# The last stage of a graph network: experts paired in the TensorE array, their third bias on VectorE, the last routing moved

## The reference, cut to what matters

```
x  = feat + wv @ Wp.T + bp
x  = x + gelu(layernorm(x)*g+b @ W1.T + b1) @ W2.T + b2      # MLP, 256 -> 1024 -> 256
xn = layernorm(x)
out = x + shared(xn) + sum over the 2 chosen experts of w_e * expert_e(xn)
shared:   relu(xn@sW1+sb1) 256->256, relu(.@sW2+sb2) ->128, .@sW3+sb3 ->256
expert_e: relu(xn@eW1+eb1) 256->128, relu(.@eW2+eb2) ->64,  .@eW3+eb3 ->256     # 4 experts
w: softmax over the 4 gate logits, the top 2, softmax of those two; 0 for the others
```

## Time and profile before

| | us |
|---|---|
| median of 3 runs | 3447.66 (3445.65 to 3448.48) |
| the profiled execution's own time | 3449.33 |
| its span | 3447.5 |
| busy: PE, PEld, DVE, ACT | 3052.7, 1592.6, 2646.8, 2136.7 |
| granted TensorE clock, mean | 0.965 |

### The profile page before, as it was taken

One profiled execution on the slowest core, in us unless ns is written; L12 is line 12 of the kernel. 1 busy time (PEld: TensorE's weight loads), 2 busy tenths in 40 slices (PEclk: granted clock), 3 DMA queues, 4 the chain that ended last, 5 costly groups with the idle time before them and its releaser, 6 DMA issues. The chain is left out here.

```text
span 3447.5 us, 43195 instructions
## 1 busy us (share of the span) xinstructions
PE 3052.7 (89%) x15721; PEld 1592.6 (46%) x15722; DVE 2646.8 (77%) x2631; ACT 2136.7 (62%) x2651; POOL 248.2 (7%) x379
## 2 busy tenths in 40 slices
PE   3776777898898988899879989999999999979998
PEld 3223333333333334788769853333333333267775
DVE  8998999799999997455442259999999999843433
ACT  3101479799999997111223359999999999834333
POOL 0000000000000000000035400101110101100000
PEclk9998999999999999999989999999999999989998
DMA  2000245677777764544176553333332333210000
GB/s 59 0 0 19 79 164 202 209 234 231 226 232 223 233 222 145 192 149 141 48 202 211 170 202 110 94 92 94 92 94 91 95 92 92 68 67 23 8 8 15
DMA packets 199234, 424.88 MB, mean 123 GB/s; under 512 B 35929, under 2 KB 133457, under 8 KB 199054
## 3 DMA queue, kind: packets, MB, share of 16 engines
q1 hardware_dynamic: 185518, 395.36, 35.8%
q0 software_dynamic: 13536, 27.08, 2.7%
HBM read 354.07 MB, written 61.88 MB: 121 GB/s over the span
## 5 line engine op out<-in xcount | busy, mean ns | idle before, releaser
L1002 PE MATMUL acc<-weights_then_messages,messages 128*64 128x391 f32 x3200 | 571.6, 505 | 81.1 <-DVE weights_then_messages L1067 74.2
L2126 PE MATMUL acc<-weights,keys_and_values 128*64 128x448 f32 x2096 | 451.2, 552 | 2.0 <-DVE weights L2289 1.9
L1002 PEld LDWEIGHTS acc<-weights_then_messages,messages 128*64 128x64 f32 x3200 | 221.3, 139 | 424.9 <-issue 273.2
L2113 PE MATMUL scores<-q,keys_and_values 32*128 32x448 f32 x2800 | 362.6, 587 | 9.5 <-ACT x L2249 4.5
L1064 DVE SCALAR_TENSOR_TENSOR weights_then_messages<-rho,kappa,counts 128x1564 f32<-128x1564 f32 x200 | 367.5, 1837 | 0.0
L1067 DVE TENSOR_TENSOR weights_then_messages<-weights_then_messages,counts 128x1564 f32<-128x1564 f32 x200 | 356.2, 1781 | 11.2 <-ACT weights_then_messages L1025 11.1
L1023 ACT ACTIVATE weights_then_messages<-rho,wx 128x1564 f32<-128x1564 f32 x200 | 317.8, 1589 | 33.2 <-PE acc L1002 31.2
L1025 ACT ACTIVATE weights_then_messages<-weights_then_messages,kappa 128x1564 f32<-128x1564 f32 x200 | 319.9, 1600 | 6.5
L674 PE MATMUL acc<-weights_then_messages 128*128 128x400 bf16 x1024 | 232.3, 359 | 85.3 <-ACT acc L650 44.2
L2286 DVE SCALAR_TENSOR_TENSOR weights<-weights,x 128x3584 f32<-128x3584 f32 x75 | 291.9, 3893 | 4.3 <-DVE weights L2279 1.1
L2251 ACT ACTIVATE weights<-scores 128x896 f32<-128x896 f32 x300 | 287.6, 981 | 10.2 <-PE scores L2113 10.2
(11 more groups left out here) (392 smaller groups left out, 4346.9 us busy)
## 6 DMA issues: line engine op xcount, KB each, us to landing
counts<-edge_counts SPq DMA_DIRECT2D x200, 782.0 KB, 4.5
x<-edge_counts SPq DMA_DIRECT2D x264, 224.0 KB, 2.7
edge_counts<-counts_out SPq DMA_DIRECT2D x40, 1000.0 KB, 4.2
counts<-edge_counts SPq DMA_DIRECT2D x24, 1600.0 KB, 7.9
w_first<-in_L_ffn_W_dram SPq DMA_DIRECT2D x57, 512.0 KB
counts<-edge_counts SPq DMA_DIRECT2D x86, 224.0 KB, 2.7
w_second<-in_L_ffn_W_dram SPq DMA_DIRECT2D x8, 512.0 KB, 8.0
normed_rows<-normed SPq DMA_DIRECT2D x5, 640.0 KB, 4.0
```

What stands on the lines that cost most here:

```text
L1002: ins = nc.tensor.matmul(acc[64 * q:64 * q + 64, m, 0:CP], message(t, head(r, q)), w[:, T % WR, q, m * CP:(m + 1) * CP], start=(t == 0), s ...
L2113: ins = nc.tensor.matmul(sc[:, (n + j // 2) % SR, j % 2, 0:CA], kT[part, r % KF, t * P:(t + 1) * P], q[part, r % 2, :], start=True, stop=True)
L2126: ins = nc.tensor.matmul(acc[64 * e:64 * e + 64, p, 0:CA], msg[:, t, r % KF * 2 + p, D * e:D * e + 2 * D], weights(U // 2)[:, 2 * p + e, U ...
```

## The change

1. The third layer's bias leaves the matmul. `e3_b` holds the four biases on all partitions (one DMA of 512 KB written, the first on SP's queue in this stage), and VectorE adds bias times weight in 20 instructions for each chunk (`add_expert_bias`); for chunks 0 to 3 they stand between the reads of the next chunk's MLP, for chunk 4 on both sides of the shared net's reads. The row of ones, its memset and TensorE's wait for it go.
2. Experts (0, 1) and (2, 3) are pairs. The second layers of a pair write PSUM partitions 0 to 63 and 64 to 127 of one bank (128 rows by 64 columns of the array each), and ScalarE reads both at once. The third layers of a pair use the array's rows 0 to 63 and 64 to 127, two banks of `down`, two reads on VectorE (`pair_down`, `finish_pair`).
3. The second pair's third layers of chunk c-2 are issued one tile at a time after halves 3 to 7 of `mlp_up` in iteration c, those of chunk 3 among the shared net's first layer in the last part. The first pair's are spread over the end of the experts (`end_moe`).
4. `norm(1, c+2)` on VectorE moves from before to behind `finish_mlp` for c = 1, 2, and its root on ScalarE behind the shared net's first layer. `norm(2)` is split: the second pair's reads stand between its statistics and its application.
5. Iteration 4: flips of chunk 4 after the shared second layer, its logits before the shared third layer, `route(4)` on VectorE right behind the shared net's reads, and its exponentials on ScalarE after entries 3 and 4 of the list.

```diff
-    MOE_UPS = [("s", 1), (0, 1), ("s", 2), (1, 1), (0, 2)] + [u for e in range(2, NE) for u in ((e, 1), (e - 1, 2))] + [(NE - 1, 2)]
+    SECOND_PAIR_AT = (3, 4, 5, 6, 7)
+    MOE_UPS = [("s", 1), (0, 1), ("s", 2), (1, 1), (2, 1), ("first", 2), (3, 1), ("second", 2)]
+    EXPERTS = {"first": (0, 1), "second": (2, 3)}
...
+        def pair_second(pe, c, pair, h):
+            n = up_no[("moe", c, pair, 2, 0, h)]
+            wait_up(pe, n)
+            pe.wait_ge(s_act, up_no[("moe", c, EXPERTS[pair][1], 1, 0, h)] + 1)
+            for i, e in enumerate(EXPERTS[pair]):
+                lanes = slice(i * P // 2, (i + 1) * P // 2)
+                ins = nc.tensor.matmul(up[lanes, n % RING, 0:TH], tw.e2[:, e, :], eh1[:, e, half(h)], start=True, stop=True)
+            ins.then_inc(s_up, 1)
...
+        def pair_down(pe, c, pair, j):
+            if j == 0:
+                pe.wait_ge(s_act, up_no[("moe", c, pair, 2, 0, 1)] + 1)
+            wait_down(pe, down_no[(EXPERTS[pair][1], c, j)])
+            for i, e in enumerate(EXPERTS[pair]):
+                n, lanes = down_no[(e, c, j)], slice(i * P // 2, (i + 1) * P // 2)
+                nc.tensor.matmul(down[:, n % RING, 0:F], eh2[lanes, e // 2, j * P:(j + 1) * P], tw.e3[lanes, e // 2, :],
+                                 start=True, stop=True).then_inc(s_down, 1)
...
+                if c and j < NE:                      # in finish_mlp, behind the read of tile j
+                    add_expert_bias(dve, c - 1, j)
...
+        def add_expert_bias(dve, c, e):
+            for j in range(TC):
+                ...
+                nc.vector.scalar_tensor_tensor(out=node, in0=e3_b[:, e, :], scalar=wf[:, c % 2, j, e:e + 1], in1=node,
+                                               op0=ALU.mult, op1=ALU.add).then_inc(s_eb, 1)
+        def finish_pair(dve, c, pair):
+            ...
+            for j in range(TC):
+                node = X[:, c * TC + j, :]
+                for i, e in enumerate(EXPERTS[pair]):
+                    n = down_no[(e, c, j)]
                     dve.wait_ge(s_down, n + 1)
+                    dve.wait_ge(s_read, n if i else down_no[("s", c, j) if pair == "first" else (EXPERTS["first"][1], c, j)] + 1)
+                    nc.vector.scalar_tensor_tensor(out=node, in0=down[:, n % RING, 0:F], scalar=wf[:, c % 2, j, e:e + 1],
+                                                   in1=node, op0=ALU.mult, op1=ALU.add).then_inc(s_read, 1)
...
             def _(sp):
+                sp.dma_start(e3_b[:, :, :].rearrange("p e f -> p (e f)"), a["L1_ffn_eb3"].rearrange("e f -> (e f)").partition_broadcast(P)
+                             ).then_inc(s_eb_in, 16)
...
             def _(pe):
                 pe.wait_ge(tw.sem, tw.count)
-                pe.wait_ge(s_row, 1)
...
+                def start_moe(c, with_pairs_of=None):
+                    for m in range(KF):
+                        for h in range(2):
+                            first_layer(pe, c, "s", m, h)
+                            if with_pairs_of is not None:
+                                pair_down(pe, with_pairs_of, "second", 2 * m + h)
+                    if with_pairs_of is not None:
+                        pair_down(pe, with_pairs_of, "second", TC - 1)
+                    for h in range(2):
+                        first_layer(pe, c, 0, 0, h)
+                    for h in range(2):
+                        shared_second(pe, c, h)
+                    if c == LAST_C - 1:
+                        for g in range(3):
+                            flip(pe, 2, LAST_C, g)
+                    for h in range(2):
+                        first_layer(pe, c, 1, 0, h)
+                    if c == LAST_C - 1:
+                        logits(pe, LAST_C)
+                    shared_down(pe, c)
+                def end_moe(c):
+                    for h in range(2):
+                        first_layer(pe, c, 2, 0, h)
+                    for h in range(2):
+                        pair_second(pe, c, "first", h)
+                    for h in range(2):
+                        first_layer(pe, c, 3, 0, h)
+                        if h == 1:
+                            pair_down(pe, c, "first", 0)
+                    pair_down(pe, c, "first", 1)
+                    for h in range(2):
+                        pair_second(pe, c, "second", h)
+                        pair_down(pe, c, "first", 2 + h)
+                    pair_down(pe, c, "first", 4)
...
+                        if n in SECOND_PAIR_AT and c >= 2:
+                            pair_down(pe, c - 2, "second", SECOND_PAIR_AT.index(n))
...
+                        start_moe(c - 1)
+                        end_moe(c - 1)
+                start_moe(LAST_C, with_pairs_of=LAST_C - 1)
+                end_moe(LAST_C)
+                for j in range(TC):
+                    pair_down(pe, LAST_C, "second", j)
...
             def _(dve):
-                nc.vector.memset(eh2[P // 2:P // 2 + 1, :, :], 1.0).then_inc(s_row, 1)
...
+                    if c:
+                        finish_shared(dve, c - 1)
+                        if c == LAST_C:
+                            route(dve, link, LAST_C)
+                        finish_pair(dve, c - 1, "first")
+                finish_pair(dve, LAST_C - 1, "second")
+                for e in range(NE // 2):
+                    add_expert_bias(dve, LAST_C, e)
+                finish_shared(dve, LAST_C, NE // 2)
+                for e in range(NE // 2, NE):
+                    add_expert_bias(dve, LAST_C, e)
+                finish_pair(dve, LAST_C, "first")
+                finish_pair(dve, LAST_C, "second")
```

More of the change, by code:

```diff
@@ L2397, in stage_tail @@
     for c in range(NTC + 1):
+        downs += [(e, c - 2, j) for j in range(TC) for e in EXPERTS["second"] if c >= 2]
         downs += [("proj", c + 2, j) for j in range(TC) if c + 2 < NTC]
         downs += [("mlp", c, j) for j in range(TC) if c < NTC]
-        downs += [(net, c - 1, j) for net in ["s"] + list(range(NE)) for j in range(TC) if c]
+        downs += [("s", c - 1, j) for j in range(TC) if c]
+        downs += [(e, c - 1, j) for j in range(TC) for e in EXPERTS["first"] if c]
+    downs += [(e, LAST_C, j) for j in range(TC) for e in EXPERTS["second"]]
     down_no = {d: n for n, d in enumerate(downs)}
@@ L2513, in mlp_up @@
             ins.then_inc(s_up, 1)
[L2515 to L2535, removed]
@@ new lines, in first_layer @@
+        def first_layer(pe, c, net, m, h):
+            n = up_no[("moe", c, net, 1, m, h)]
+            wait_up(pe, n)
+            if net == "s" and m == 0 and h == 0:
+                pe.wait_ge(s_turn, flip_no[(2, c, 2)] + 1)
+            for k in range(KF):
+                w = tw.s1[:, k, m * P:(m + 1) * P] if net == "s" else tw.e1[:, net, k, :]
+                ins = nc.tensor.matmul(up[:, n % RING, 0:TH], w, XT[:, k, columns(c, h)], start=(k == 0), stop=(k == KF - 1))
+            ins.then_inc(s_up, 1)
@@ new lines, in shared_second @@
+        def shared_second(pe, c, h):
+            n = up_no[("moe", c, "s", 2, 0, h)]
+            wait_up(pe, n)
+            pe.wait_ge(s_act, up_no[("moe", c, "s", 1, KF - 1, h)] + 1)
+            for k in range(KF):
+                ins = nc.tensor.matmul(up[:, n % RING, 0:TH], tw.s2[:, k, :], sh1[:, k, half(h)], start=(k == 0), stop=(k == KF - 1))
+            ins.then_inc(s_up, 1)
+        def pair_second(pe, c, pair, h):
+            n = up_no[("moe", c, pair, 2, 0, h)]
+            wait_up(pe, n)
+            pe.wait_ge(s_act, up_no[("moe", c, EXPERTS[pair][1], 1, 0, h)] + 1)
+            for i, e in enumerate(EXPERTS[pair]):
+                lanes = slice(i * P // 2, (i + 1) * P // 2)
+                ins = nc.tensor.matmul(up[lanes, n % RING, 0:TH], tw.e2[:, e, :], eh1[:, e, half(h)], start=True, stop=True)
+            ins.then_inc(s_up, 1)
@@ L2693, in add_shared_bias @@
             nc.vector.tensor_tensor(nodes, nodes, tw.s3_b[:, :].unsqueeze(1).to_broadcast([P, TC, F]), ALU.add).then_inc(s_sb, 1)
[L2695 to L2701, removed]
-                    dve.wait_ge(s_down, n + 1)
[L2703 to L2709, removed]
+        def add_expert_bias(dve, c, e):
+            for j in range(TC):
+                node = X[:, c * TC + j, :]
+                if e:
+                    dve.wait_ge(s_eb, (c * NE + e - 1) * TC + j + 1)
+                else:
+                    dve.wait_ge(s_sb, c + 1)
+                if c == LAST_C and e == NE // 2:
+                    dve.wait_ge(s_read, down_no[("s", c, j)] + 1)
+                nc.vector.scalar_tensor_tensor(out=node, in0=e3_b[:, e, :], scalar=wf[:, c % 2, j, e:e + 1], in1=node,
+                                               op0=ALU.mult, op1=ALU.add).then_inc(s_eb, 1)
@@ L2827, in _ @@
                     norm(dve, 1, c)
+                dve.wait_ge(s_eb_in, 16)
                 for c in range(NTC):
                     if c:
-                        norm(dve, 2, c - 1)
+                        norm_stats(dve, 2, c - 1)
```

(3 more changed lines are left out.)

118 lines of the change are left out of this document (53 added, 65 removed).

## The result

The changed kernel took 3420.74 us (median of 4 runs, 3417.02 to 3425.31) against 3446.65 for the kernel before on the same chip: ratio 0.9924, 95% interval 0.9908 to 0.9941. Two more sets of runs gave 3425.09 (0.9939, 0.9923 to 0.9956) and 3421.97 (0.9926, 0.9914 to 0.9938). These two stand against 3446.65 and 3448.11 for the kernel before on their own chips. So it is 22 to 26 us less, against 28.8 by the sum of the prediction, whose forecast was 3419.

The account below looks back on a forecast made before the run. From iteration 1 on TensorE was taken as the bound, by passes, exposed weight loads or idle time. Terms -7.4, -5.85, -3.45, +3.45, -18.85 and +3.3 sum to -28.8 us, against the median 3447.66: 3419, range 3407 to 3437.

Parts of the forecast that it names:

- Nets of a chunk: A chunk's nets without the second pair's third layers: 24.7 us, 6.9 below 31.58.
- Second pair in `mlp_up`: Second pair's third layers add 4.15 us in the next `mlp_up`; the root's stall of 0.7 there goes.
- Last routing: Iteration 4's nets, with chunk 4's routing within them: end at 28.3 us against 47.15, -18.85.
- Last part: From iteration 4's nets to the last read: 36.8 us against 33.5, 3.3 longer with chunk 3's second pair.
- Biases and norm cost nothing: VectorE's biases and moved norm(1) are covered by TensorE; without cover, up to 2 us in each of two iterations.
- `mlp_down` of iteration 1: MLP's second layer in iteration 1: -0.5 us, up to -2.5, part of its loss being low clock.
- Start: Stage's start: memset of 2.19 us goes, `e3_b` DMA may delay loads 0 to 2; gain 0 to 2, taken as 0.
- rival (a): Low clock after gate logits and at the last part's end: +6.8 and +3 us, 3429; chance 0.17.
- (b): Iteration 4: VectorE reaches the last routing late, TensorE idles about 5, low spell 8.3: +13 us, 3432; chance 0.08.
- (c): Experts' pairs take three slots instead of two: 3.2 us a chunk, +16 in all, 3435; chance 0.05.
- (d): Second and third layers' 70 pairs don't overlap, four slots each: +47 us, 3466, slower than before; chance 0.05.
- The 15 for exposed weights: Part of (d), in pairs without overlap: weights exposed at each change of half (0.21) add 15 us more.

Follow-up runs that it names:

- e3_b: Not a run: the buffer with the four third-layer biases on all partitions, written by one DMA of 512 KB; no time of its own.
- the kernel with one half: Changed kernel with both members of a pair in the same half of the array: 3450.78 us, ratio 1.0012 to the kernel before.
- the move alone: Kernel before with only the last chunk's routing moved (flips, logits, route, exponentials): 3437.34 us, ratio 0.9977 to the kernel before.
- norm back: Changed kernel with the first norm of chunks 3 and 4 back before the adds and the MLP's reads, its root before the nets: 3430.09 us.
- exponentials late: Changed kernel with chunk 4's two exponentials back late in ScalarE's list, after expert 3's first layer in iteration 4: 3428.46 us.

## Why the prediction was right, step by step

- **Nets of a chunk**: 24.7 forecast, 24.5 to 24.6 measured. Passes, 18 changes of shape at 0.2 and the wait of 1.28 between bare pairs (measured 1.26) were right. Overlap of row halves, for which no row of before stood, is shown by the kernel with one half (1.06 for a pair against 0.63).
- **Second pair in `mlp_up`**: +4.15 less 0.7 for the root's stall, 3.45; iteration 2's stretch from the nets' end to `mlp_down` went from 26.47 to 30.14, +3.67. Iterations 2 and 3 as a whole: -5.85 and -3.45 forecast, -5.60 and -3.28 measured.
- **Last routing**: 28.3 forecast, 28.43 measured. The first pair's read was to be due 1.3 us after route's end; it came 1.67 after it (3364.69 and 3366.36). Of the 18.7 won there, 10.4 belong to the move alone.
- **Last part**: 36.8 forecast, 37.09 (3371.52 to 3408.61).
- **Biases and norm cost nothing**: shown, each by its own run, though for the biases in the last part the proof is weaker, as said above; the norm's old place costs 2.3 an iteration.
- **`mlp_down` of iteration 1**: mis-sized. I took -0.5 and said that the rest was a low spell. It was -2.3. The stall and the spell lay over each other: with VectorE's first read as the limit, 19.66 comes out at either clock, in iteration 1 with a spell and in iteration 2 without.
- **Start**: mis-sized. I took 0; it was +1.8 (26.03 to 27.79). The bias DMA ahead of the loads costs 3.4 to 3.9, where I had allowed 0 to 2, and leaving out the memset brought 1.4 (one execution). In the profile after, the first load, issued at 3020.76, is in the chain with 5.80 us; before, it took 4.1. The rest of the cost is the low clock behind it, which the sum did not have.
- These two errors are of 1.8 each and cancel, which is luck: -28.8 forecast, -28.34 in the stage.
- **Medians**: 22 to 26, because of rival (a) in part. A low spell in `mlp_down` costs 1.7 or 2.5 to 3.0. Before, one that came early in iterations 1 or 2 was hidden under the stall, as in the profile before; now each counts.
- **What leads to the spells** is supported by counts and not settled. In the nine profiles of the kernels with pairs and the gate matmuls in one stretch, a spell fell in 16 of 36 `mlp_down`s, and in the three with them spread in none of the ten that were spread. But 13 of the 16 fell in iterations 3 and 4, where TensorE also waits for ScalarE ahead of the gate matmuls, a wait that spreading shortens, and one of the other three came behind the stall (norm back). So in iterations 1 and 2, without that wait, a spell came right behind the gate matmuls in 2 of 18, and what the wait adds was not tested apart. The last chunk's gate matmuls, in one stretch everywhere and with a short wait in the flips ahead of them, had a low spell right behind them in five of these twelve profiles. Why one execution is hit and the next is not stays open.
- **The other rivals**: (b) did not come, and with exponentials late it can be seen. (c), three slots a pair, would be 0.64 and a change of shape; the third layers take 0.63 with their change. (d) was priced too high: with no overlap the stage is 25 to 29 us longer and not 47. The 15 for exposed weights did not come (1.06 - 0.63 is just the two slots more), and a chunk's nets grew by 3.4 where the added slots alone would be 4.3.

## What to carry to other kernels

Price an overlap of small matmuls with its changes of array shape and its bank waits: here passes fell by 6.4 us a chunk, and 3.1 of it went back to those in iteration 3, which fell by 3.28. When a stall goes, look at what lay hidden under it, here spells of low clock. Look at what a new DMA stands ahead of. And look first for the one late wait behind which the clock falls: moving one routing step brought 12 of 28 us in the profiles (9.3 of 21.6 by medians), for the smallest edit.

## What was not expected of the hardware

Ten gate matmuls of 4 columns take 2.13 us in one stretch and 3.1 when put between full matmuls, yet the clock was at 1.00 over 345 us in the profile of the second way. A DMA of 512 KB ahead of the first load delayed the stage by 3.4 to 3.9 us, more than the 2.4 us by which that load came later, and TensorE, which had idled longer for it, then ran part of the projection at the low clock (0.76 on average over 5.96 us, against 1.00 over 4.58).
